# Five dense units moved from the kept steps into the list steps of a graph layer; tail roots and normalising one slot later

## The chip, the cores and the metric

The kernel runs on one core of one Trainium2 chip. The metric is the device time of one execution in microseconds (us); a lower time is better. Each time given as "median of the runs" is over unprofiled runs; the trace comes from one more execution, taken by the hardware profiler.

## What is computed

```python
x = setup()                         # (100000, 256) f32; 25000 edges, sorted by dst
def _spmm(edge_src, edge_dst, edge_weight, feats, n_nodes):
    msgs = edge_weight[:, None] * feats[edge_src]
    return jax.ops.segment_sum(msgs, edge_dst, num_segments=n_nodes)
feats = [x]; cur = x
for _ in range(3):
    cur = _spmm(src, dst, edge_weight, cur, n_nodes)
    feats.append(cur)
y = jnp.concatenate(feats, axis=1) @ shared_weight + output_bias   # weight (1024, 256)
out = layernorm(x + y)              # over the 256 columns, no gain or bias
```

Every node needs x times the first 256 rows of the weight, plus x, plus bias, and a layernorm: that is the **dense** part. Only nodes with edges need more, and only some edges reach a second and third hop: that is the **sparse** part, which ends in a gather and a scatter of single rows of the output.

## The kernel before

**Dense units.** The 100000 rows are cut into 195 units of 512 rows (128 partitions x 4 rows) and a tail. A unit is loaded by SP's queue (512 KB), turned on TensorE (`turn_pair`, L1472), copied to SBUF by ScalarE (`copy_xT`, L1185), multiplied on TensorE (`multiply_part`, L1483), copied out with the bias by VectorE (`copy_y`, L1840), measured there (`unit_stats`, L1846; `unit_end` with the lines 1855, 1851 and 1861), rooted and normalised by ScalarE (L1189, L1198) and stored by SP's queue (512 KB). A unit is two pairs, and each pair passes each of these engines once. VectorE's share of a unit is two `copy_y`, four `bn_stats` and three small instructions.

**Steps and slots.** The program is written out by hand, engine by engine, as steps of eight slots (q = 0 to 7). Each step carries a piece of the sparse part and a fixed number of dense units, which the tables of sizes set: one (ONE), two (PAIR), three (STEP) or four (FOUR). Within a step the tables `PAIR_AT`, `ROOTS_AT` and `ROWS_AT` say at which slot an engine does which pair. Every engine runs its own queue in that order and waits on semaphores; nothing is reordered at run time. The units go through the stages in one sequence:

- 25 `a` steps of two units (first hop, and the table of edges with a second hop);
- 10 **list steps** of one unit (`list_step`, L514). In the last six, five of which are called `LIST_STEPS`, the active edges are compacted into a list: VectorE makes indices for a group of 4 x 127 entries (`pass_tiles` L2213, `stage_list` L2223/L2224), POOL issues four indirect DMAs for it (`list_group` L973, the DMAs show as L917 with the tile `entries`), VectorE takes the landed entries (`take_entries` L2232 to L2240). Between these VectorE computes pointers in 40 small pieces (`find_pointers`, L2250 to L2301), each of which waits for the one before it;
- `bridge_b` (three units), five `b` steps of four units (second hop), `bridge_c`;
- ten `c` steps of one or two units (third hop; some early tail tiles), `bridge_d`;
- the **D steps** d = 3 to 23, four units each. A tile is 128 tails (last edge of a node). In the **kept steps**, d = 3 to 19, POOL gathers the eight tiles' rows from the stored output (`gather_d`, L917 tile `rows_in`), VectorE undoes their normalising and adds the sparse result (`c_restore` L2702), measures it (`c_stats` L2707, `group_squares` L2601, `group_variance` L2607), ScalarE takes the root for a group of four tiles (`c_roots` L1401), VectorE the inverse (`c_inverse` L2712), ScalarE normalises a tile (`c_normalise` L1408, output tile `u_out`), and POOL scatters it into the output (`scatter_d` L1110, shown as L921). From step 20 on the rows come from x and are turned and multiplied again on TensorE (L1751, L1757).

**Distances.** At slot n of the D steps (n = 8d + q) POOL issues the gather of tile n + 4 (which waits until tile n - 4 is restored) and the scatter of tile n - 12, which begins at n = 36, the middle of step 4; VectorE restores tile n - 2, which waits until ScalarE has normalised tile n - 10; ScalarE normalises tile n - 8, which waits for the scatters of the pair of tiles eight before it, since `u_out` holds eight tiles.

Of the kernel before, what the change touches and what calls it, by code (L numbers as in the profile page):

```python
def gnn_program(nc, x, src, dst, edge_weight, weight, bias, out):
# [23 lines left out]
    STEP = 3  # L25
    RING = 2 * STEP
    PAIR, FOUR = 2, 4
# [4 lines left out]
    G = 4  # L32
    Q = 2 * G
    FULL = E // EPT
    REST = E - FULL * EPT
    REAL = FULL + 1
# [16 lines left out]
    LIST_UNIT = A_UNIT + PAIR * A_STEPS  # L53
    LIST0 = 4
    LIST_STEPS = 5
    LIST_ALL = LIST0 + LIST_STEPS + 1
    ONE = 1
    B_UNIT = LIST_UNIT + ONE * LIST_ALL + STEP
    B_STEPS = LIST_STEPS
    BRIDGE_UNIT = B_UNIT + FOUR * B_STEPS  # L60
    FIRST_GROUPS = 2 * LIST_STEPS
# [4 lines left out]
    E_STEPS = E_QUADS * G // Q  # L66
    EARLY = Q * E_STEPS
# [4 lines left out]
    D_STEPS = REAL // Q  # L72
# [5 lines left out]
    GROUPS_MIN = FIRST_GROUPS + 1  # L78
    GROUPS_MAX = TILES // G
    LATE0 = Q * D_STEPS  # L80
    D_SIZES = (0,) * E_STEPS + (FOUR,) * (D_STEPS - E_STEPS)
    D_OFFS = tuple(D_UNIT + sum(D_SIZES[:d]) for d in range(D_STEPS))
    FRESH_UNIT = D_OFFS[KEPT_STEPS]
    assert D_UNIT + sum(D_SIZES) == UNITS

# [44 lines left out]
    with ctx:  # L130
# [202 lines left out]
        turns_at = {}  # L333
# [170 lines left out]
        def unit_at(off, turns=0):  # L504

            return off + RING * turns, off % RING, turns + off // RING, off % STEP
# [5 lines left out]
            return A_UNIT + PAIR * i, PAIR, turns, STEP if isinstance(turns, int) and i == 0 else PAIR  # L512

        def list_step(l):  # L514
            return LIST_UNIT + ONE * l, ONE, 0, PAIR

        def b_step(b):
            return B_UNIT + FOUR * b, FOUR, 0, FOUR if b > 0 else STEP


        bridge_b = (B_UNIT - STEP, STEP, 0, ONE)
        bridge_c = (BRIDGE_UNIT, STEP, 0, FOUR)
# [5 lines left out]
        def d_step(d):  # L528
            return D_OFFS[d], D_SIZES[d], 0, D_SIZES[d - 1] if d > E_STEPS else FOUR

# [639 lines left out]
        def _(act):  # L1170

            PAIR_AT = {FOUR: {q: q for q in range(Q)}, STEP: {0: 0, 1: 1, 2: 2, 4: 3, 5: 4, 6: 5},
                       PAIR: {0: 0, 2: 1, 4: 2, 6: 3}, 1: {0: 0, 4: 1}}

            ROOTS_AT = {FOUR: {1: -1, 3: 0, 5: 1, 7: 2}, STEP: {2: -1, 4: 0, 7: 1}, PAIR: {2: -1, 6: 0}, 1: {4: -1}}
            ROWS_AT = {FOUR: {0: (-3, 1), 1: (-2, 0), 2: (-2, 1), 3: (-1, 0), 4: (-1, 1), 5: (0, 0), 6: (0, 1), 7: (1, 0)},
                       STEP: {0: (-3, 1), 2: (-2, 0), 3: (-2, 1), 4: (-1, 0), 5: (-1, 1), 7: (0, 0)},
# [3 lines left out]
            def copy_xT(p, rows=P):  # L1181
                act.wait_ge(xT_psum, p + 1)
                until(act, y_psum, columns_before[p] + 1)
                view = [t[:, :].rearrange("p (q c) -> p q c", c=P)[:, :, 0:rows] for t in (columns_in[p], turned_in[p])]
                act.copy(view[0], view[1]).then_inc(xT_copied, 1)  # L1185

            def roots(u, k, rows=P, tiles=RPP):
                act.wait_ge(var_ready, u + 1)
                act.activation(std_all[0:rows, RPP * u:RPP * u + tiles], squares[k][0:rows, 0:tiles], ACT.Sqrt,  # L1189
                               scale=1.0 / D, bias=eps[0:rows, :]).then_inc(std_ready, 1)  # L1190

            def normalise(u, k, slot, turn, half, rows=P):

                if half == 0:
                    act.wait_ge(rstd_ready, u + 1)
                    until(act, stored[slot], 16 * turn)
                for r in (2 * half, 2 * half + 1):
                    last = act.activation(o_ring[slot][0:rows, r * D:(r + 1) * D], y_ring[k][0:rows, r * D:(r + 1) * D],  # L1198
                                          ACT.Copy, scale=rstd[k][0:rows, r:r + 1])
                if half == 1 or rows < P:  # L1200
                    last.then_inc(normed, 1)

            def dense_slot(dense, q):
                off, units, turns, before = dense

                def has_rows(i):

                    return i >= -off and (i > -3 or before >= STEP)

                if q in ROWS_AT[units] and ROWS_AT[units][q][0] == -3 and has_rows(-3):  # L1210
                    u, slot, turn, k = unit_at(off - 3, turns)
                    normalise(u, k, slot, turn, 1)
                if off >= D_UNIT:
                    if off == D_UNIT and q == 0:
                        copy_xT(LAST_PAIR)
                    for p in turns_at.get(2 * off + q, ()):
                        copy_xT(p)
                elif q in PAIR_AT[units]:
                    copy_xT(2 * off + PAIR_AT[units][q])
                if q in ROOTS_AT[units] and has_rows(ROOTS_AT[units][q]):  # L1220
                    u, slot, turn, k = unit_at(off + ROOTS_AT[units][q], turns)
                    roots(u, k)
                if q in ROWS_AT[units]:
                    i, half = ROWS_AT[units][q]
                    if i > -3 and has_rows(i):
                        u, slot, turn, k = unit_at(off + i, turns)
                        normalise(u, k, slot, turn, half)
# [134 lines left out]
            for n in range(G * FIRST_GROUPS):  # L1362
                g, k = n // G, n % G
# [39 lines left out]
            def c_normalise(n, q, group, turn):  # L1403
                act.wait_ge(crstd_ready, group + 1)
                if q % 2 == 0:
                    until(act, scattered[q // 2], 32 * turn)
                half, k = q // G, q % G
                act.activation(co[q], cy[q], ACT.Copy, scale=crstd[half][:, k:k + 1]).then_inc(cnormed, 1)  # L1408

            def step_d(d, slot=None):  # L1410

                for q in range(Q):
                    n, g = Q * d + q, 2 * d + q // G
                    if KEPT <= n < REAL:
                        copy_ta(n, q)
                    if slot is not None:
                        slot(q)
                    if q % G == 2 and 2 * E_STEPS < g <= -(-REAL // G):
                        c_roots(g - 1, (q // G + 1) % 2)
                    if Q + EARLY <= n < REAL + Q:  # L1420
                        c_normalise(n - Q, q, g - 2, d - 1)

            def last_units(q):
                u = UNITS
# [391 lines left out]
        def _(dve):  # L1816
# [545 lines left out]
            for b in range(LIST_STEPS):  # L2362
                dense = list_step(LIST0 + b)
                for q in range(Q):
                    g = 2 * b + 2 + q // G
# [9 lines left out]
            for q in range(G):  # L2375
                if q % 2 == 0:
                    g = FIRST_GROUPS - 2 + q // 2
# [247 lines left out]
            for n in range(G * FIRST_GROUPS):  # L2625
                g, k = n // G, n % G
# [32 lines left out]
            LAST_GROUP = (REAL - 1) // G  # L2659
# [49 lines left out]
            def c_inverse(g, half):  # L2709
                dve.wait_ge(cstd_ready, g + 1)  # L2710
                until(dve, cnormed, G * (g - 1))
                dve.reciprocal(crstd[half][:, :], cstd[half][:, :]).then_inc(crstd_ready, 1)  # L2712

            def step_d(d, par, turn, copies=None, measures=None):
                for q in range(Q):
                    n, g, half = Q * d + q, 2 * d + q // G, q // G
                    real = 2 + EARLY <= n < REAL + 2
                    measured = 3 + EARLY <= n < REAL + 3
                    if measured and (q % G == 2 or n == REAL + 2):
                        dve.wait_ge(cstats_ready, n - 2)  # L2720
                        group_squares((n - 3) // G, (n - 3) % G + 1)
                    if real:
                        before = q < 2
                        part = 2 * ((par + before) % 2) + (q - 2) % Q // G
                        if n - 2 < KEPT:
                            c_restore(n - 2, (q - 2) % Q, d - before, part, turn - 1 if before and par == 0 else turn)
                        else:
                            c_copy(n - 2, (q - 2) % Q, part, turn - 1 if before and par == 0 else turn)
                    if copies is not None:
                        copies(q)  # L2730
                    if n < KEPT and q < 2:
                        (pick_std, sum_picked)[q](d)
                    if real:
                        c_stats(n - 2, (q - 2) % Q)
                    for s in range(1, len(SPLITS)):
                        if SPLITS[s][0] == d and q < 4:
                            split_std(s, q)
                    if d + 1 < KEPT_STEPS and q in (2, 3):
                        mark_parts(d + 1, q - 2)
                    if d + 1 < KEPT_STEPS and q == 5:  # L2740
                        mark_cols(d + 1)
                    if measures is not None:
                        measures(q)
                    if measured and (q % G == 2 or n == REAL + 2):
                        group_variance((n - 3) // G, (n - 3) % G + 1)
                    if q % G == 3 and 2 * E_STEPS + 1 <= g <= LAST_GROUP + 1:
                        c_inverse(g - 1, 1 - half)

            last_step = (UNITS, STEP, 0, STEP)

# [72 lines left out]
```

## Time and profile before

| | us |
|---|---|
| median of 3 runs | 1538.12 (1538.0 to 1543.98) |
| the profiled execution | 1543.04, of which the span is 1541.0 |

| engine | busy us | share of the span |
|---|---|---|
| TensorE (PE) | 1417.6 | 92% |
| VectorE (DVE) | 1177.7 | 76% |
| POOL (GpSimd) | 1072.4 | 70% |
| ScalarE (ACT) | 998.6 | 65% |

The span is the time from the first to the last instruction, 2.0 us less than the execution's own time. The shares are averages over stages with very different limits. A DMA that POOL issues shows as an instruction of about 1 us on POOL, which is the issuing alone; what it moves shows in the DMA columns. In the views of time, an instruction's start is followed by how long it took; two instructions of one engine can overlap by some tens of ns, so the cost of one in a row of them is the distance from start to start.

### The profile page before, as it was taken

Reading aid. Unit: us, or ns where it says so; the run is one execution under the profiler, and the core shown is the slowest. Engines: PE = TensorE matmul, PEld = TensorE weight load, DVE = VectorE, ACT = ScalarE, POOL = GpSimd, SP = SyncE. Lnnn points to the kernel's source line nnn. Section 1 sums busy time; section 2 is a strip of 40 time slices with the busy share of each in tenths; the row PEclk is TensorE's granted clock in tenths of the full one; section 3 lists DMA queues with packets and bytes.
Section 4 is the critical chain, followed back from the end, with each engine's and each line's share of the span. In section 5 each row is a group of like instructions: output and inputs, shape, how many; then the busy total and the mean of one; then the engine's idle time right before and its main releaser. Section 6 shows DMA issues by size and latency. Waiting matters only on the chain. (4 is left out here: it accounts for less than half of the span.)

```text
span 1541.0 us, 29919 instructions
## 1 busy us (share of the span) xinstructions
PE 1417.6 (92%) x7990; PEld 1209.9 (79%) x7990; DVE 1177.7 (76%) x4195; ACT 998.6 (65%) x2674; POOL 1072.4 (70%) x1046
## 2 busy tenths in 40 slices
PE   6999999999999986689989999989998998888995
PEld 5888888888888875578878878878777777767884
DVE  8777777777777777978763766549999999997664
ACT  4677777777777753257764555646777776666665
POOL 4577777777777754747755877873777777777744
PEclk9999999999999999799999999999999999999997
DMA  7788988888888875378976877769999999998863
GB/s 260 248 259 275 281 280 281 266 272 282 281 279 265 274 239 182 99 237 311 334 271 166 239 231 199 205 175 326 341 349 344 342 338 337 332 338 295 301 204 124
DMA packets 214319, 410.69 MB, mean 267 GB/s; under 512 B 30996, under 2 KB 137485, under 8 KB 214154
## 3 DMA queue, kind: packets, MB, share of 16 engines
q1 hardware_dynamic: 164582, 311.03, 59.0%
q0 software_dynamic: 48576, 97.04, 22.2%
q8 instruction: 67, 1.10, 0.3%
q10 hardware_dynamic: 996, 0.72, 0.2%
q14 instruction: 98, 0.80, 0.2%
HBM read 227.02 MB, written 193.96 MB: 273 GB/s over the span
## 5 line engine op out<-in xcount | busy, mean ns | idle before, releaser
L1483 PE MATMUL ps_y<-w_sb,xT 128*128 128x256 f32 (+1 forms) x1928 | 501.3, 389 | 14.7 <-DVE y_ring L1840 12.5
L1483 PEld LDWEIGHTS ps_y<-w_sb,xT 128*128 128x128 f32 (+1 forms) x1928 | 353.3, 195 | 55.7 <-issue 9.1
L1198 ACT ACTIVATE o_ring<-y_ring,rstd 128x256 f32<-128x256 f32 (+1 forms) x782 | 350.3, 498 | 0.0
L1840 DVE TENSOR_TENSOR y_ring<-ps_y,bias 128x512 f32<-128x512 f32 (+1 forms) x325 | 224.0, 689 | 150.1 <-PE ps_y L1483 136.8
L1846 DVE BATCH_NORM_STATS2 stats<-y_ring 128x6 f32<-128x256 f32 (+1 forms) x782 | 291.2, 414 | 4.2
L917 POOL DMA_INDIRECT rows_in<-in_x,gather_idx x200 | 202.5, 1013 | 87.6 <-issue 66.5
L917 POOL DMA_INDIRECT tails_found<-tail_keys,table_idx x200 | 201.2, 1006 | 79.5 <-issue 58.2
L921 POOL DMA_INDIRECT out_rows<-u_out,early_node x173 | 178.4, 1031 | 80.6 <-issue 39.8
L917 POOL DMA_INDIRECT rows_in<-out_rows,early_node x160 | 166.9, 1043 | 73.2 <-issue 39.3
L1568 PE MATMUL ps_u<-w_sb,cT 128*128 128x256 f32 x788 | 206.2, 384 | 0.3 <-DVE u_out L2084 0.3
L1472 PE MATMUL ps_xT<-ident,x_ring 128*128 128x128 f32 x1140 | 177.8, 280 | 13.1 <-ACT xT L1185 8.0
L1247 ACT COPY rows_in<-ps_sum 1x256 f32<-1x256 f32 x282 | 101.1, 358 | 128.3 <-PE ps_sum L1546 73.3
L1185 ACT COPY xT<-ps_xT 128x512 f32<-128x512 f32 x254 | 145.3, 572 | 58.3 <-PE ps_xT L1472 58.2
L1472 PEld LDWEIGHTS ps_xT<-ident,x_ring 128*128 128x128 f32 x1140 | 140.2, 144 | 37.3 <-ACT xT L1185 10.7
L1483 PE MATMUL ps_sum<-w_sb,xT 128*128 128x256 f32 x528 | 138.6, 388 | 19.9 <-ACT xT L1185 19.9
L1568 PEld LDWEIGHTS ps_u<-w_sb,cT 128*128 128x128 f32 x788 | 141.8, 190 | 16.3 <-issue 1.0
L2084 DVE COPY u_out<-ps_u 128x512 f32<-128x512 f32 x80 | 55.3, 691 | 96.8 <-PE ps_u L1568 56.6
L1483 PEld LDWEIGHTS ps_sum<-w_sb,xT 128*128 128x128 f32 x528 | 93.8, 192 | 39.7 <-ACT xT L1185 30.6
L1546 PE MATMUL ps_sum<-rows_in,sels 128*128 128x256 f32 x394 | 119.9, 386 | 5.2 <-ACT rows_in L1247 4.3
L1189 ACT ACTIVATE std_all<-squares,eps 128x4 f32<-128x4 f32 x196 | 58.4, 298 | 90.1 <-DVE squares L1861 88.0
L1408 ACT ACTIVATE u_out<-sums,crstd 128x256 f32<-128x256 f32 x173 | 86.0, 500 | 44.5 <-DMA out_rows<-u_out,early_node 42.7
L1483 PE MATMUL ps_y<-w_sb,xT_more 128*128 128x256 f32 x336 | 89.5, 390 | 7.1 <-ACT xT_more L1185 7.0
(365 smaller groups left out, 2595.2 us busy)
## 6 DMA issues: line engine op xcount, KB each, us to landing
x_ring<-in_x SPq DMA_DIRECT2D x195, 512.0 KB, 5.9
out_rows<-o_ring SPq DMA_DIRECT2D x195, 512.0 KB, 4.4
c_rows<-sums SPq DMA_DIRECT2D x49, 512.0 KB
u_rows<-u_out SPq DMA_DIRECT2D x49, 512.0 KB, 5.1
keys_bc<-u_rows SPq DMA_DIRECT2D x21, 512.0 KB, 7.3
listed<-u_rows SPq DMA_DIRECT2D x14, 512.0 KB, 5.6
c_list_rows<-sums SPq DMA_DIRECT2D x11, 512.0 KB
u_out<-c_list_rows SPq DMA_DIRECT2D x44, 128.0 KB, 4.7
```

The lines of the kernel that those rows point to most:

```text
L917: pool.indirect_dma_start(dest, None, table, bass.IndirectOffsetOnAxis(ap=index, axis=0), bounds_check=bound, oob_is_err=False).then_inc(s ...
L921: pool.indirect_dma_start(table, bass.IndirectOffsetOnAxis(ap=index, axis=0), source, None, bounds_check=bound, oob_is_err=False).then_inc ...
L1185: act.copy(view[0], view[1]).then_inc(xT_copied, 1)
L1198: last = act.activation(o_ring[slot][0:rows, r * D:(r + 1) * D], y_ring[k][0:rows, r * D:(r + 1) * D], ACT.Copy, scale=rstd[k][0:rows, r:r ...
L1247: act.copy(rows_in[row][0:1, :], last_row).then_inc(carry_ready, tiles)
L1408: act.activation(co[q], cy[q], ACT.Copy, scale=crstd[half][:, k:k + 1]).then_inc(cnormed, 1)
L1472: last = pe.transpose(bank[:, q * P:q * P + rows], x_ring[slot][0:rows, at:at + P], ident[0:rows, 0:rows])
L1483: last = pe.matmul(y_bank[p][0:rows, r * D:(r + 1) * D], columns_in[p][:, q * P:q * P + rows], w_sb[:, c, :], start=c == 0, stop=c == KC - 1)
L1546: pe.matmul(ps_sum[e // 2 % 2][:, e % 2 * D:(e % 2 + 1) * D], sel[q % G][:, :], rows_in[q][:, :], start=True, stop=True).then_inc(summed, ...
L1568: last = pe.matmul(ps_u[1][:, r * D:(r + 1) * D], cT[j % 2][:, at:at + P], w_sb[:, KC + c, :], start=c == 0, stop=c == KC - 1)
L1840: dve.tensor_tensor(y_ring[k][0:rows, half * 2 * D:(half + 1) * 2 * D], y_bank[p][0:rows, :], bias2[0:rows, :], ALU.add).then_inc(y_copied, 1)
L1846: last = dve.bn_stats(stats[k][0:rows, r, :], y_ring[k][0:rows, r * D:(r + 1) * D])
```

## The change

Three edits go together.

1. The five `LIST_STEPS` carry two units instead of one (`L_SIZES`). All later stages up to the kept steps therefore work on units whose number is five higher; their sizes stay.
2. The kept steps 4, 8, 12, 16 and 19 carry three units instead of four (`LIGHT_STEPS`). For those ScalarE gets a table, `TURNED_AT`, of the slots at which TensorE has turned a pair. From step 20 on every unit stands where it stood.
3. On ScalarE the root of a group of tails moves from slot 2 (or 6) to slot 3 (or 7), and at slot n tile n - 9 is normalised instead of n - 8. On VectorE `c_inverse` is written at the start of a slot instead of at the end of the one before it, which is the same place in its queue.

```diff
+    L_SIZES = (ONE,) * LIST0 + (PAIR,) * LIST_STEPS + (ONE,)
-    B_UNIT = LIST_UNIT + ONE * LIST_ALL + STEP
+    B_UNIT = LIST_UNIT + sum(L_SIZES) + STEP
...
-    D_SIZES = (0,) * E_STEPS + (FOUR,) * (D_STEPS - E_STEPS)
+    LIGHT_STEPS = (4, 8, 12, 16, 19)
+    D_SIZES = (0,) * E_STEPS + tuple(STEP if d in LIGHT_STEPS else FOUR for d in range(E_STEPS, D_STEPS))
...
         def list_step(l):
-            return LIST_UNIT + ONE * l, ONE, 0, PAIR
+            return LIST_UNIT + sum(L_SIZES[:l]), L_SIZES[l], 0, PAIR
...
+            TURNED_AT = {FOUR: {q: q for q in range(Q)}, STEP: {1: 0, 2: 1, 3: 2, 5: 3, 6: 4, 7: 5}}
...
-                    for p in turns_at.get(2 * off + q, ()):
+                    done = TURNED_AT[units].get(q)
+                    for p in turns_at.get(2 * off + done, ()) if done is not None else ():
                         copy_xT(p)
...
-                    if q % G == 2 and 2 * E_STEPS < g <= -(-REAL // G):
+                    if q % G == G - 1 and 2 * E_STEPS < g <= -(-REAL // G):
                         c_roots(g - 1, (q // G + 1) % 2)
-                    if Q + EARLY <= n < REAL + Q:
-                        c_normalise(n - Q, q, g - 2, d - 1)
+                    m = n - Q - 1
+                    if EARLY <= m < REAL:
+                        c_normalise(m, m % Q, m // G, m // Q)
...
+                    if q % G == 0 and 2 * E_STEPS + 2 <= g <= LAST_GROUP + 2:
+                        c_inverse(g - 2, half)
...
-                    if q % G == 3 and 2 * E_STEPS + 1 <= g <= LAST_GROUP + 1:
-                        c_inverse(g - 1, 1 - half)
```

How VectorE's queue reads in the second half of a list step, first before (here `sums` and `own` are pieces of the pointers, `passes_out`, `entries` and `list_idx` the making of the indices, `y_ring`, `stats`, `rstd` and `squares` a dense unit):

```order
L2213 SCALAR_TENSOR_TENSOR passes_out,passed<-ends,position,skips 128x201 x4
L2273 TENSOR_TENSOR sums<-sums 128x256
L2223 COPY entries<-blank_entries 128x36
L2224 TENSOR_TENSOR list_idx<-list_row,passed 128x4
L2273 TENSOR_TENSOR sums<-sums 128x256 x2
L2276 SCALAR_TENSOR_TENSOR own,begun_before<-ident,sums 128x128
L1840 TENSOR_TENSOR y_ring<-ps_y,bias 128x512
L1846 BN_STATS stats<-y_ring 128x6 x2
L1855 SCALAR_TENSOR_TENSOR stats<-stats 128x8
```

and the same stretch of VectorE's queue after (line numbers are five higher):

```order
L2218 SCALAR_TENSOR_TENSOR passes_out,passed<-ends,position,skips 128x201 x4
L2278 TENSOR_TENSOR sums<-sums 128x256
L2228 COPY entries<-blank_entries 128x36
L2229 TENSOR_TENSOR list_idx<-list_row,passed 128x4
L2278 TENSOR_TENSOR sums<-sums 128x256
L1845 TENSOR_TENSOR y_ring<-ps_y,bias 128x512
L1851 BN_STATS stats<-y_ring 128x6 x2
L1860 SCALAR_TENSOR_TENSOR stats<-stats 128x8
L1856 RECIPROCAL rstd<-std_all 128x4
L1866 TENSOR_REDUCE squares<-stats 128x4
L2278 TENSOR_TENSOR sums<-sums 128x256
```

Every half step now holds two pairs of a dense unit where it held one; nothing else of VectorE's list work has gone.

ScalarE's queue in a kept step of four units, slots 2 to 4, before (`xT1` and the like are turned pairs, `o_ring` a dense unit's output, `cstd` the tails' root, `u_out` a normalised tail tile):

```order
L1198 ACTIVATE o_ring5<-y_ring2,rstd2 128x256 x2
L1401 ACTIVATE cstd1<-csquares1,eps 128x4
L1408 ACTIVATE u_out<-sums,crstd0 128x256
L1185 COPY xT1<-ps_list 128x512
L1189 ACTIVATE std_all<-squares1,eps 128x4
L1198 ACTIVATE o_ring0<-y_ring0,rstd0 128x256 x2
L1408 ACTIVATE u_out<-sums,crstd0 128x256
```

and after:

```order
L1201 ACTIVATE o_ring5<-y_ring2,rstd2 128x256 x2
L1412 ACTIVATE u_out<-sums,crstd0 128x256
L1188 COPY xT_more<-ps_list 128x512
L1192 ACTIVATE std_all<-squares1,eps 128x4
L1201 ACTIVATE o_ring0<-y_ring0,rstd0 128x256 x2
L1405 ACTIVATE cstd1<-csquares1,eps 128x4
L1412 ACTIVATE u_out<-sums,crstd0 128x256
```

The tails' root stands behind the next turned pair and the next dense root, and so does what follows it.

## Rows read from the trace of the kernel before

**Rows 1.** Busy time by stretch: list steps, kept steps, last steps (x instructions).
```profile
core 0: us, PE busy (x) PEld busy (x) DVE busy (x) ACT busy (x) POOL busy (x), PEclk, DMA share, GB/s
601.00:659.00 58.00, 36.65 (x144) 27.88 (x144) 54.99 (x244) 17.68 (x42) 44.46 (x44) 0.85 0.37 106
1077.00:1398.00 321.00, 287.93 (x1799) 236.95 (x1798) 309.98 (x968) 226.68 (x575) 248.26 (x239) 0.99 0.97 339
1404.00:1515.00 111.00, 110.26 (x601) 95.94 (x602) 75.68 (x244) 75.04 (x197) 66.16 (x67) 0.98 0.73 247
```

**Rows 2.** Waits in the list steps, 601 to 659: total us, times, longest.
```profile
DVE sums L2255 <- DVE next_f L2253: 0.5, 1, 0.5
...
POOL entries L917 <- DVE list_idx L2224: 13.5, 1, 13.5
POOL entries L917 <- issue: 13.1, 43, 0.3
```

**Rows 3.** VectorE in a list step, a unit's first pair, and another unit's second.
```profile
635.13 0.69 DVE L1840 TENSOR_TENSOR y_ring<-ps_y,bias 128x512 f32<-128x512 f32 x1
...
636.52 0.15 DVE L2232 SCALAR_TENSOR_TENSOR key_in<-entries 128x4 f32<-128x4 f32 x1
...
640.32 0.69 DVE L1840 TENSOR_TENSOR y_ring<-ps_y,bias 128x512 f32<-128x512 f32 x1
...
642.12 0.15 DVE L2232 SCALAR_TENSOR_TENSOR key_in<-entries 128x4 f32<-128x4 f32 x1
```

**Rows 4.** Waits of POOL and of VectorE in the kept steps, 1077 to 1398.
```profile
POOL rows_in L917 <- issue: 27.9, 91, 0.3
POOL out_rows L921 <- issue: 27.7, 91, 0.3
...
POOL rows_in L917 <- ACT u_out L1408: 3.3, 10, 0.6
...
DVE sums L2702 <- ACT u_out L1408: 6.4, 7, 2.5
```

**Rows 5.** POOL in step 4, where the scatters begin, in order of time.
```profile
1073.26 1.00 POOL L917 DMA_INDIRECT rows_in<-out_rows,early_node  x1 [1.58 <-DVE sums L2702]
1074.56 1.02 POOL L921 DMA_INDIRECT out_rows<-u_out,early_node  x1 [0.30 <-issue]
1076.13 1.03 POOL L917 DMA_INDIRECT rows_in<-out_rows,early_node  x1 [0.55 <-ACT u_out L1408]
```

**Rows 6.** VectorE in a kept step, a unit's second pair and what follows it.
```profile
1185.04 0.74 DVE L1846 BATCH_NORM_STATS2 stats<-y_ring 128x6 f32<-128x256 f32 x2
1185.71 0.15 DVE L2601 SCALAR_TENSOR_TENSOR cstats<-cstats 128x8 f32<-128x8 f32 x1
...
1186.17 0.68 DVE L1840 TENSOR_TENSOR y_ring<-ps_sum,bias 128x512 f32<-128x512 f32 x1
1186.77 0.41 DVE L2707 BATCH_NORM_STATS2 cstats<-sums 128x6 f32<-128x256 f32 x1
1187.11 0.73 DVE L1846 BATCH_NORM_STATS2 stats<-y_ring 128x6 f32<-128x256 f32 x2
1187.87 0.17 DVE L1855 SCALAR_TENSOR_TENSOR stats<-stats 128x8 f32<-128x8 f32 x1
...
1188.16 0.16 DVE L2607 TENSOR_REDUCE csquares<-cstats 128x4 f32<-128x16 f32 x1
```

**Rows 7.** The first VectorE instruction of kept steps 4, 7 and 19.
```profile
1067.46 0.61 DVE L2669 TENSOR_TENSOR sels<-ps_u,matches 128x448 f32<-128x448 f32 x1
...
1128.49 0.61 DVE L2669 TENSOR_TENSOR sels<-ps_u,matches 128x448 f32<-128x448 f32 x1
...
1383.49 0.62 DVE L2669 TENSOR_TENSOR sels<-ps_u,matches 128x448 f32<-128x448 f32 x1
```

**Rows 8.** The chain that ended last, where the kept steps end: start, us, what.
```profile
1397.67 7.03 DMA rows_in<-in_x,tail_node
...
1404.74 0.69 PE ps_u L1751 x2
```

## The prediction

> **What bounds the kernel now.** I read the busy time of the stretches that the change touches first, then who waited for whom in each, then the order of time at the places where one engine hands over to another.
>
> *The list steps* [rows 1] take 58 us. VectorE is busy for 54.99 us of them, so it is full. POOL is nearly full too, in another way: it issues 44 gathers of list entries, busy 44.46 us, plus a fixed 0.3 us between two of them, 13.1 us in all [rows 2], together 57.6 us. After the first gather it never waits for VectorE (the 13.5 us stand before that gather), and VectorE's one wait of note is 0.5 us [rows 2]; its whole idle time is 58 - 54.99 = 3.0 us. So two engines run through this stage side by side at the same pace, and neither has room. TensorE has: 36.65 us of 58. ScalarE has: 17.68.
>
> *The kept steps* [rows 1] look full everywhere: VectorE 309.98 of 321 us, TensorE 287.93, DMA share 0.97 at 339 GB/s. What orders them is the waits. POOL issues 239 DMAs in 321 us, one each 1.343 us; 248.26 us are busy, and its waits are the same 0.3 us before every instruction, whatever released it [rows 4]. The longest is 0.6 us. It is the 0.3 us that also stands between list gathers that wait for nothing, so it is the price of an issue and no wait. POOL has therefore no idle moment from 1077 to 1398 us. A kept step has 16 of its instructions (8 gathers, 8 scatters), which makes 16 x 1.343 = 21.5 us. VectorE alone would be faster: from step 4 to step 7 a step took (1128.49 - 1067.46) / 3 = 20.34 us, and from step 7 to step 19 (1383.49 - 1128.49) / 12 = 21.25 us [rows 7]. In the first part POOL fell behind by using up its lead; in the second VectorE was held to POOL's pace, through ScalarE, which waits for scatters to land before it overwrites a tile (VectorE's 6.4 us in 7 waits for `u_out` [rows 4]).
>
> *The last steps* begin when POOL's gather of tile 160, the first row of step 20, has landed: issued at 1397.67, 7.03 us under way, and TensorE starts at 1404.74 [rows 8]. From there TensorE is full, 110.26 of 111 us [rows 1]. So the chain to the end is: list steps, a TensorE-full stage, the third hop, POOL from 1077 to 1398, TensorE from 1405.
>
> **The list steps after.** Each of five steps gets one unit more. VectorE pays for a unit's first pair 636.52 - 635.13 = 1.39 us and for its second, with the three small instructions, 642.12 - 640.32 = 1.80 us, start to start [rows 3], so 3.19 us for a unit and 5 x 3.19 = **15.95 us** in all. I place all of it on the path, because VectorE's only real gap is that 0.5 us. Its bounds: if all 3.0 us of idle time were filled, 13.0; if it cost what it costs in a kept step (below), 14.6; if it met a new wait of up to the 0.5 us above in each step, 18.5. Of the other engines none is late: POOL's 57.6 us become less than VectorE's 58 + 16 = 74; TensorE's 36.65 us grow with its instructions, 5/10 more dense work even if all of it were dense and at half clock twice that, to at most 36.65 x 2 = 73, and the granted clock was 0.85 here, so it is more likely near 55; ScalarE doubles to 35 at most. The 10 added transfers of 512 KB make 5.2 MB beside the 106 GB/s x 58 us = 6.1 MB of now, in 74 us, 154 GB/s, less than half of the 339 of the kept steps. The gathers of entries and the indices that VectorE makes two groups ahead of POOL now wait for VectorE instead of the other way about; that is where the queue behind the added work shows. The pointers, the entries and everything behind them start some 16 us later. If POOL set this stage alone, the added work would be hidden; the busy time of VectorE speaks against it.
>
> **The kept steps after.** A unit costs VectorE there 0.60 + 0.67 us for the first pair (a copy start to start, 1186.77 - 1186.17, and the measuring, 1185.71 - 1185.04) and 0.60 + 0.76 + 0.29 for the second (1187.87 - 1187.11, 1188.16 - 1187.87) [rows 6], 2.92 us. Five units are 14.6 us of VectorE's time, and about as much of TensorE's. Only what VectorE was late with counts. Before the first scatter POOL waited for VectorE at every gather: 1.58 us at 1073.26, and 0.55 us still at 1076.13 [rows 5]. Those gathers wait for tiles 32 and 33, restored in slots 2 and 3 of step 4. In a light step slot 0 has no pair, so one pair less stands ahead of them: 1.27 us for the first, 1.65 for the second. POOL's own spacing then allows 1073.26 - 1.27 + 2 x 1.30 = 1074.6 instead of 1076.13, which is **1.5 us** gained. From there POOL issues without a wait, as now; the rest of step 4's unit and the whole of the units of steps 8, 12, 16 and 19, 13.1 us of VectorE's time, turn into waiting of VectorE and TensorE for POOL. Bounds: nothing gained at all, 0; everything, 14.6. I take 1.5, since the saved pairs after 1077 have no reader that was late for them.
>
> **Roots and normalising one slot later.** This has one cover: POOL's pace. ScalarE normalises tile n - 9 at slot n, still before POOL scatters n - 12, so POOL does not wait. VectorE restores n - 2 one slot after ScalarE has finished n - 10, where it had two slots. A slot is 21.25 / 8 = 2.66 us, and ScalarE's work in it, 226.68 us in some 121 slots, is 1.9 us, so it is just in time. For the other sign: ScalarE no longer stands at slot 2 for a root that VectorE finishes at the end of slot 2, and has one slot more for a scatter to land. I count 0; if each of the 34 groups of four tiles met one wait like the mean of the seven of now (6.4 / 7 = 0.9 us), 31 us would be added to VectorE, of which POOL's lead hides 15 x 0.9 us and the light steps 11.7, leaving up to 6. In the last steps the tail tiles are normalised by the same queue in the same order; between 0 and one slot of TensorE's, 3.25 us, I take 0, since VectorE is busy there 75.68 of 111 us.
>
> **Sum**, against the profiled execution: 1543.04 + 15.95 - 1.5 + 0 = 1557.5 us, so +14.4. The median of the runs is 4.9 us below that execution; 1538.1 + 14.4 gives **1552.5 us**, +0.94%.
>
> **A rule that speaks for the change.** The kept steps move 339 GB/s with a DMA share of 0.97 [rows 1]. If the bytes set their pace, each unit taken out (512 KB in, 512 KB out, 1.049 MB) gives 1.049 / 0.339 = 3.1 us, five of them 15.5. The Trainium skill, "DMA: Bandwidth & Descriptors", Specifications, puts the limit of the memory per core at about 358 GB/s, of which the measured 339 is 95%; by that rule the kept steps are bound by bandwidth. It is rival A below, under its own price. What speaks against it is POOL's row: an engine that issues each DMA 0.3 us after the last has not been held by transfers, and it has the larger sum.
>
> **The rivals.**
> A. *The kept steps give it back.* VectorE, TensorE or the bytes set the pace there, and POOL only follows. Then 14.6 to 15.5 us return: 1538.1 + 15.95 - 14.6 = 1539.5 (1538.6 by the bytes), no change. For it: VectorE's 97% and the DMA share. Against it: steps 7 to 19 ran 0.9 us slower than VectorE can. It decides from the point where POOL's 21.5 us a step fall below VectorE's 20.3.
> B. *The list steps hide it*, VectorE's pieces of pointers being in truth paced by the landing of entries: then the stage stays at 58 us and the time is 1536.6, or 1523.5 with A. Against it: no wait on `entries` is listed for VectorE.
> C. *The later normalising stalls the restores*, up to 6 us more: 1558.5.
> D. *Half of A*, POOL slack in part: about 1545.5.
>
> **Chances.** The forecast 0.70 (1547 to 1557), A 0.09 (1536 to 1543), D 0.07 (1543 to 1547), B 0.06 (1522 to 1538), C 0.08 (1556 to 1562). The range 1540 to 1557 leaves out B, most of C and part of A, about 0.17. About 0.5% (7.7 us, 1530.4 to 1545.8) is what a measurement of this kernel can tell from no change. Slower by more: the forecast, C and half of D, 0.80. Within it: A, the rest of D and a part of B, 0.15. Faster by more: B with A, 0.05.
>
> **What would show it.** In the changed kernel's profile the list steps should take about 74 us instead of 58, with VectorE full and POOL waiting for `list_idx` in most groups. In the kept steps POOL should again show only 0.3 us before each instruction, 16 instructions a step at 21.3 to 21.6 us, with VectorE's and TensorE's idle time up by some 13 us together with waits for `u_out` or for landed rows; the distance from the first scatter to the gather of tile 160 should be what it was, 1397.67 - 1074.56 = 323 us. The wait of TensorE for tile 160 should be longer. Wrong would be the forecast if that distance fell by more than 5 us (A), if the list steps grew by less than 10 us (B), or if POOL showed waits for `u_out` of over 0.3 us in the kept steps (C).

## The result, and the profile after

| | before | after |
|---|---|---|
| median of the runs, us | 1539.18 (1534.91 to 1544.06, 6 runs) | 1555.54 (1553.32 to 1558.34, 6 runs) |
| the profiled execution, us (its span) | 1543.04 (1541.0) | 1556.87 (1554.8) |

The changed kernel is slower: the ratio is 1.0098, with a 95% interval from 1.0081 to 1.0115, some 15 us (the two medians lie 16.4 us apart). The forecast was +14.4 us and 1552.5 us.

I cut both traces at the same five events and compare the pieces. (`sels` is the instruction of [rows 7]; in a step whose slot 0 holds a dense pair, the copy of that pair stands 0.6 us ahead of it.) The pieces add up to the difference of the two spans, 13.8 us.

| piece, from and to | before | after | difference | forecast |
|---|---|---|---|---|
| start to the first `list_idx` of the list | 599.65 | 601.36 | +1.7 | 0 |
| list: to the last `take_entries` | 62.10 | 77.77 | **+15.67** | +15.95 |
| second and third hop: to the `sels` instruction of step 3 on VectorE | 386.63 | 385.49 | -1.1 | 0 |
| to the first scatter (step 4) | 26.18 | 24.93 | **-1.25** | -1.5 |
| kept steps: first scatter to the gather of tile 160 | 323.11 | 322.32 | **-0.8** | 0 |
| gather of tile 160 to the end | 143.33 | 142.93 | -0.4 | 0 |

*The list steps.* Busy time by stretch after, which answers to [rows 1]: list steps, kept steps, last steps.

```profile
core 0: us, PE busy (x) PEld busy (x) DVE busy (x) ACT busy (x) POOL busy (x), PEclk, DMA share, GB/s
603.00:676.00 73.00, 53.17 (x263) 42.40 (x264) 69.55 (x285) 32.42 (x77) 43.84 (x44) 0.98 0.50 155
1092.00:1412.00 320.00, 275.76 (x1698) 228.79 (x1696) 299.04 (x931) 217.47 (x548) 247.27 (x239) 0.96 0.95 330
1419.00:1530.00 111.00, 111.00 (x611) 96.46 (x609) 78.30 (x250) 74.72 (x196) 65.09 (x65) 0.99 0.71 237
```

And the waits from 603 to 677 us after, which answer to [rows 2] (total us, times, longest):

```profile
POOL entries L919 <- DVE list_idx L2229: 25.3, 7, 14.2
...
POOL entries L919 <- issue: 11.5, 37, 0.5
...
DVE sums L2260 <- DVE next_f L2258: 0.5, 1, 0.5
```

VectorE is busy for 69.55 of 73 us and still has one wait, of 0.5 us. Its idle time is 3.45 us, where it was 3.0 of 58: the added work filled no gap and met no new wait. POOL changed sides. Before, one wait of 13.5 us stood ahead of its first gather and nothing but 0.3 us behind it; now it waits seven times for the indices, and 25.3 - 14.2 = 11.1 us of that lie behind the first gather. TensorE (36.65 to 53.17) and ScalarE (17.68 to 32.42) took their share in idle time that they had. VectorE after, a whole unit and then a unit's second pair (start, us), as in [rows 3]:

```profile
631.08 0.68 DVE L1845 TENSOR_TENSOR y_ring<-ps_y,bias 128x512 f32<-128x512 f32 x1
...
634.27 0.15 DVE L2237 SCALAR_TENSOR_TENSOR key_in<-entries 128x4 f32<-128x4 f32 x1
...
636.52 0.69 DVE L1845 TENSOR_TENSOR y_ring<-ps_y,bias 128x512 f32<-128x512 f32 x1
...
638.32 0.41 DVE L2275 COPY sums<-ps_sum 128x255 f32<-128x255 f32 x1
```

A unit, 634.27 - 631.08 = 3.19 us, costs here what [rows 3] gave; its second pair, 638.32 - 636.52 = 1.80 us, too.

*The kept steps.* Waits from 1092 to 1412 us after, which answer to [rows 4]:

```profile
ACT std_all L1192 <- DVE squares L1866: 71.9, 51, 2.3
...
POOL rows_in L919 <- issue: 27.9, 91, 0.3
POOL out_rows L923 <- issue: 27.1, 89, 0.3
...
DVE sums L2707 <- ACT u_out L1412: 16.0, 17, 2.3
...
POOL rows_in L919 <- ACT u_out L1412: 4.0, 13, 0.3
```

POOL issues the same 239 DMAs and never waits longer than the 0.3 us that stand before every one of them. Its own pace stayed: from its gather of tile 60 to that of tile 156, twelve steps, a step took 21.58 us before (1127.82 to 1386.81) and 21.57 after (1142.28 to 1401.06). VectorE has 320 - 299.04 = 21.0 us idle where it had 11.0, and its waits for `u_out` have grown from 6.4 to 16.0 us: the same 10 us. TensorE's idle time went from 33.1 to 44.2 us. So the work that left became waiting for POOL. The handovers, on POOL, VectorE and TensorE, which answer to [rows 5], [rows 7] and [rows 8]:

```profile
1083.09 0.62 DVE L2674 TENSOR_TENSOR sels<-ps_u,matches 128x448 f32<-128x448 f32 x1
1142.97 0.61 DVE L2674 TENSOR_TENSOR sels<-ps_u,matches 128x448 f32<-128x448 f32 x1
1397.07 0.62 DVE L2674 TENSOR_TENSOR sels<-ps_u,matches 128x448 f32<-128x448 f32 x1
```

```profile
1088.25 1.00 POOL L919 DMA_INDIRECT rows_in<-out_rows,early_node  x1 [1.99 <-DVE sums L2707]
1089.55 1.24 POOL L923 DMA_INDIRECT out_rows<-u_out,early_node  x1 [0.30 <-issue]
...
1411.87 1.02 POOL L919 DMA_INDIRECT rows_in<-in_x,tail_node  x1 [0.31 <-issue]
...
1417.48 0.69 PE L1756 MATMUL ps_u<-ident,rows_in 128*128 128x128 f32 x2 [6.71 <-DMA rows_in<-in_x,tail_node]
```

On VectorE the `sels` of steps 4, 7 and 19 begin at 1083.09, 1142.97 and 1397.07. From 7 to 19 a step took 21.18 us, with three light steps (8, 12 and 16) among the twelve, where it was 21.25 with none. Of these 0.9 us in all, 0.6 are the copy of a pair that light step 19 lacks ahead of its `sels`. From the first scatter to the gather of tile 160 are 322.32 us. That is 0.8 us less than before, and no gain can be read from it: the kernels below that keep four units in every kept step and POOL's queue as it is (the third edit alone, the fewer bytes, and the three of the last two experiments) took 320.5 to 322.5 us over the same piece. TensorE waits 6.71 us for the row of tile 160, where it waited 2.93.

### The profile page after: what moved, and what is told of

Its sections match the earlier page's. It is cut to its first block and busy times, and to the rows that moved or that the text cites. A ratio compares the mean times of both kernels' runs of the same rounds, so it can differ in the third digit from the quotient of the medians.

```text
span 1554.8 us, 29919 instructions
## 1 busy us (share of the span) xinstructions
PE 1416.8 (91%) x7990; PEld 1212.0 (78%) x7990; DVE 1179.5 (76%) x4195; ACT 1001.6 (64%) x2674; POOL 1068.7 (69%) x1046
## 5 line engine op out<-in xcount | busy, mean ns | idle before, releaser
L1488 PE MATMUL ps_y<-w_sb,xT 128*128 128x256 f32 x2496 | 645.7, 388 | 31.4 <-ACT xT L1188 24.4
L1488 PEld LDWEIGHTS ps_y<-w_sb,xT 128*128 128x128 f32 x2496 | 453.8, 194 | 87.5 <-ACT xT L1188 32.1
L1845 DVE TENSOR_TENSOR y_ring<-ps_y,bias 128x512 f32<-128x512 f32 (+1 forms) x331 | 228.0, 689 | 144.1 <-PE ps_y L1488 130.9
L1477 PE MATMUL ps_xT<-ident,x_ring 128*128 128x128 f32 x1164 | 180.8, 279 | 22.0 <-ACT xT L1188 16.4
L1188 ACT COPY xT<-ps_xT 128x512 f32<-128x512 f32 x261 | 149.5, 573 | 70.7 <-PE ps_xT L1477 70.6
L1477 PEld LDWEIGHTS ps_xT<-ident,x_ring 128*128 128x128 f32 x1164 | 141.8, 143 | 47.8 <-ACT xT L1188 21.5
L1239 ACT ACTIVATE sign_out<-first_keys,source_key 128x197 bf16<-128x197 f32 x200 | 90.6, 453 | 0.0
L1049 POOL DMA_INDIRECT u_rows<-u_out,scatter_idx x44 | 70.3, 1598 | 23.8 <-issue 14.7
L1551 PEld LDWEIGHTS ps_sum<-rows_in,sels 128*128 128x128 f32 x394 | 73.2, 192 | 16.0 <-issue 5.0
```

The costliest lines, as they stand in the source:

```text
L1477: last = pe.transpose(bank[:, q * P:q * P + rows], x_ring[slot][0:rows, at:at + P], ident[0:rows, 0:rows])
L1488: last = pe.matmul(y_bank[p][0:rows, r * D:(r + 1) * D], columns_in[p][:, q * P:q * P + rows], w_sb[:, c, :], start=c == 0, stop=c == KC - 1)
L1551: pe.matmul(ps_sum[e // 2 % 2][:, e % 2 * D:(e % 2 + 1) * D], sel[q % G][:, :], rows_in[q][:, :], start=True, stop=True).then_inc(summed, ...
L1845: dve.tensor_tensor(y_ring[k][0:rows, half * 2 * D:(half + 1) * 2 * D], y_bank[p][0:rows, :], bias2[0:rows, :], ALU.add).then_inc(y_copied, 1)
```

## The experiments

Ratios are to the kernel before on the same chip, with a 95% interval. Times of pieces are from one profiled execution each, cut as in the table above. Where nothing is said of the list, it took 62.0 to 62.1 us with one unit a step and 77.7 with two.

**The third edit alone.** The kernel before, with roots and normalising one slot later and no unit moved.

```diff
-                    if q % G == 2 and 2 * E_STEPS < g <= -(-REAL // G):
+                    if q % G == G - 1 and 2 * E_STEPS < g <= -(-REAL // G):
                         c_roots(g - 1, (q // G + 1) % 2)
-                    if Q + EARLY <= n < REAL + Q:
-                        c_normalise(n - Q, q, g - 2, d - 1)
+                    m = n - Q - 1
+                    if EARLY <= m < REAL:
+                        c_normalise(m, m % Q, m // G, m // Q)
...
```

> The kernel before with only the third edit: tail roots and normalising one slot later. My theory (POOL's issuing covers ScalarE's order): no change, within 2 us. Rival C (the restores stall on the later normalising): up to 6 us slower, with VectorE waiting for u_out at most groups. A gain of over 3 us would say that the roots' stalls on ScalarE had been on the path.

1541.69 us, ratio 1.000 (0.9986 to 1.0014). The edit costs nothing and gains nothing, within 2 us. Yet the trace shows that it moved waits about; from 1077 to 1398 us:

```profile
ACT std_all L1189 <- DVE squares L1862: 75.2, 60, 2.2
...
ACT u_out L1408 <- DMA out_rows<-u_out,early_node: 10.3, 13, 1.7
...
DVE sums L2703 <- ACT u_out L1408: 5.0, 8, 1.5
```

ScalarE's wait for landed scatters was 40.9 us in 26 before and is 10.3 now, and its 49.5 us of waiting for the tails' squares (25 waits of `cstd`) are gone from the list; it waits for dense squares instead, 75.2 us for 1.4. VectorE's wait for `u_out` is 5.0 us where it was 6.4. Rival C, a stall of the restores by this edit, is out for the kernel before.

**The moved units alone.** The changed kernel with the third edit taken back.

```diff
-                    if q % G == G - 1 and 2 * E_STEPS < g <= -(-REAL // G):
+                    if q % G == 2 and 2 * E_STEPS < g <= -(-REAL // G):
                         c_roots(g - 1, (q // G + 1) % 2)
-                    m = n - Q - 1
-                    if EARLY <= m < REAL:
-                        c_normalise(m, m % Q, m // G, m // Q)
+                    if Q + EARLY <= n < REAL + Q:
+                        c_normalise(n - Q, q, g - 2, d - 1)
...
```

> The changed kernel without the third edit: only the five units move. My theory: all of the loss is here, +14 to +16 us against the kernel before, list steps some 16 us longer, kept steps at most 1.5 us shorter. If the later normalising had been part of the loss (or of a hidden gain), this run is faster (or slower) than the changed kernel by that.

1555.07 us, ratio 1.0081 (1.006 to 1.0102). The list took 77.74 us, the piece to the first scatter 24.94 (26.18 before) and the kept steps 321.43. The whole loss is in the moved units; what the third edit adds to them is 0.0017 in the ratio (1.0098 - 1.0081), inside either interval.

**One small DMA more on POOL in each kept step.** If POOL has no idle moment, a DMA that nobody needs must lengthen the stage by its issue.

```diff
                         scatter_d(n - LAG, (q + G) % Q, d - back, (par + back) % 2)
+                    if q == Q - 1 and 5 <= d < KEPT_STEPS:
+                        pool.wait_ge(list_in[0], 16 * G * 3 + 16 * (d - 5))
+                        limit(P * TILES)
+                        gather(entries[0][:, 0:FIELDS], list_dram, list_idx[0][:, 0:1], list_in[0])
```

> The kernel before with one more indirect DMA on POOL in each of the 15 kept steps from 5 to 19, which gathers 128 rows of 36 bytes (4.6 KB, nobody reads them). POOL theory: each costs its full issue, 15 x 1.34 = +20 us. If VectorE or the bytes set the pace (rival A), next to nothing, under +3 us, until POOL's slack of theirs is used up.

1560.03 us, ratio 1.0123 (1.0098 to 1.0147). The kept steps took 341.64 us for 323.11, with 14 DMAs more up to the gather of tile 160: 18.5 / 14 = 1.32 us each. The whole execution took 17 to 19 us more, for the 20 expected. POOL around one of them:

```profile
1217.69 1.01 POOL L921 DMA_INDIRECT out_rows<-u_out,early_node  x1 [0.30 <-issue]
1219.01 1.29 POOL L917 DMA_INDIRECT entries<-listed_edges,list_idx  x1 [0.31 <-issue]
1220.60 1.00 POOL L917 DMA_INDIRECT rows_in<-out_rows,early_node  x1 [0.30 <-issue]
```

The added DMA moves little, but it costs a full issue, 1220.60 - 1219.01 = 1.59 us at this place and 1.32 in the mean, and none of it is hidden. This alone doesn't tell whether less work on POOL would help; the next but one does.

**Fewer bytes.** The 56 units from step 6 to step 19 load only one of each partition's four rows, 128 KB for 512, 22 MB less in all. The rest of these units is computed from what the buffer held, so that part of the output is not the layer's.

```diff
-                sp.dma_start(x_ring[slot][:, :], unit_rows(x, u)).then_inc(x_loaded[slot], 16)
+                if D_OFFS[6] <= u < D_OFFS[KEPT_STEPS]:
+                    rows = x[bass.ds(u * UROWS, UROWS), :].rearrange("(p r) d -> p r d", r=RPP)
+                    sp.dma_start(x_ring[slot][:, 0:D].rearrange("p (r d) -> p r d", r=1), rows[:, 0:1, :]).then_inc(x_loaded[slot], 16)
+                else:
+                    sp.dma_start(x_ring[slot][:, :], unit_rows(x, u)).then_inc(x_loaded[slot], 16)
```

> The kernel before, with 56 units of the kept steps loading a quarter of their rows (128 KB instead of 512 KB; the other rows are what the buffer held, so part of the output is computed from old rows). 22 MB less are moved, every engine's instructions stay. POOL theory and VectorE theory: no change, within 3 us. If the bytes set the pace of the kept steps: 22 MB at 339 GB/s would be 65 us, of which VectorE's 20.34 us a step lets 11 to 12 us through: -11 us or more.

1540.7 us, ratio 0.9989 (0.9973 to 1.0004), and the kept steps took 322.02 us. The same stretch, 1095 to 1375 us, of the kernel before and then of this one:

```profile
1095.00:1375.00 280.00, 252.04 (x1590) 207.65 (x1590) 270.93 (x847) 198.81 (x504) 216.43 (x209) 0.99 0.97 340
```

```profile
1095.00:1375.00 280.00, 256.28 (x1622) 212.99 (x1622) 273.87 (x857) 202.18 (x513) 216.43 (x209) 0.99 0.82 269
```

The DMA share fell from 0.97 to 0.82 and the rate from 340 to 269 GB/s, and POOL issued the same 209 DMAs in the same 280 us. The bytes don't set the pace.

**Half of the scatters left out, in the kernel before.** From tile 41 to tile 151 every other scatter isn't issued, 56 of them, so that POOL has room; the rows of those tiles keep what the dense part wrote.

```diff
-                scatter(out[:, :], co[q], early_node[:, n:n + 1], scattered[q // 2])
+                if q % 2 == 1 and Q * 5 <= n < KEPT - Q:
+                    pool.reg_add(bound, nought, N - 1)
+                elif q % 2 == 0 and Q * 5 <= n < KEPT - Q:
+                    pool.indirect_dma_start(out[:, :], bass.IndirectOffsetOnAxis(ap=early_node[:, n:n + 1], axis=0), co[q], None,
+                                            bounds_check=bound, oob_is_err=False).then_inc(scattered[q // 2], 32)
+                else:
+                    scatter(out[:, :], co[q], early_node[:, n:n + 1], scattered[q // 2])
```

> The kernel before without the scatters of every second tail tile from tile 41 to 151 (56 indirect DMAs left out; those rows keep their dense value). POOL then has 12 instructions a step, 16.1 us. POOL theory: the pace falls to VectorE's 20.34 us a step, 0.9 us less in each of steps 7 to 19, -11 us, and no further, since VectorE is next. If VectorE set the pace already: 0 to -2 us.

1530.26 us, ratio 0.9921 (0.9895 to 0.9947), 11 to 12 us less, as expected. Its kept steps took 306.14 us with 187 DMAs for 239. Busy time and POOL's first wait from 1095 to 1375 us, and two step starts of VectorE:

```profile
1095.00:1375.00 280.00, 257.70 (x1641) 213.25 (x1641) 278.10 (x875) 203.77 (x519) 178.21 (x171) 1.00 0.96 332
```

```profile
POOL rows_in L917 <- DVE sums L2708: 48.8, 40, 1.9
```

```profile
1212.24 0.62 DVE L2675 TENSOR_TENSOR sels<-ps_u,matches 128x448 f32<-128x448 f32 x1
...
1252.96 0.61 DVE L2675 TENSOR_TENSOR sels<-ps_u,matches 128x448 f32<-128x448 f32 x1
```

Now POOL waits for VectorE, in 40 places, and VectorE is busy for 278.10 of 280 us. Two steps took 40.72 us, 20.36 each, which is the 20.34 of [rows 7] that the prediction took for VectorE's own pace. 52 DMAs less are 70 us of POOL's time, of which the stage got 17: VectorE stands right behind POOL. ScalarE's waits for landed scatters and VectorE's for `u_out` are both gone from the list of waits of this window. The 17 us have two parts. VectorE's twelve steps from 7 to 19 took 8.7 us less (20.53 a step in the mean, for 21.25). And POOL, which in the kernel before issued its gather of tile 156 3.3 us after VectorE's `sels` of step 19, issued it here 4.2 us ahead of it, 7.5 us more. The piece behind the gather of tile 160 grew by 3.2 us (143.33 to 146.50), which is why the whole execution gained 12 us and not 17.

**The same scatters left out of the changed kernel.** If POOL's pace was what held the light steps' gain back, this kernel must come close to the one before it.

```diff
+                if q % 2 == 1 and Q * 5 <= n < KEPT - Q:
+                    pool.reg_add(bound, nought, N - 1)
...
```

> The changed kernel with the same 56 scatters left out. With POOL out of the way its light steps should now give back their units: against e5 +16 us for the list steps and -14.6 us for the kept steps, so e6 and e5 within 3 us of each other, where the changed kernel and the kernel before are 15 us apart. If the light steps are worth little whatever POOL does, e6 stays 12 to 16 us above e5.

1535.81 us, ratio 0.9962 (0.9945 to 0.998): 5.5 us above the last experiment, where the same change cost 15 to 16 us with all scatters. The kept steps took 298.55 us for 306.14, the piece to the first scatter 24.94 for 26.18: 8.8 us came back. From 1095 to 1375 us:

```profile
1095.00:1375.00 280.00, 250.00 (x1596) 208.71 (x1594) 276.04 (x864) 198.83 (x507) 183.63 (x176) 0.99 0.96 329
```

```profile
POOL rows_in L919 <- ACT u_out L1418: 39.4, 33, 1.8
...
DVE sums L2713 <- ACT u_out L1418: 2.0, 3, 0.7
```

```profile
1171.32 0.48 DVE L2713 SCALAR_TENSOR_TENSOR sums<-rows_in,row_std,keys_bc 128x256 f32<-128x256 f32 x1 [0.68 <-ACT u_out L1418]
```

So with room on POOL more than half of the light steps' 14.6 us comes back, and with POOL full hardly any does. The size was missed: I expected this kernel within 3 us of the other, so 13 us or more back. A light step gave back about 2 us where the sum had 2.92. VectorE is no longer quite full (4.0 us idle in 280, for 1.9), and the list names where: it now waits three times for ScalarE's `u_out`, 0.7 us each, once in each of the light steps 8, 12 and 16 (the row above is step 8), where the last experiment lists no such wait. From the `sels` of step 7 to that of step 18, with these three light steps between them, VectorE took 219.66 us for 225.49, 5.8 less where 3 x 2.92 = 8.8 were to come; the waits make up 2.0 of the 2.9 us that are missing. POOL stands for `u_out` in 33 places, where it stood for VectorE; the left-out scatters still wait for their tile, so part of these waits belongs to them. That the later normalising is behind both is likely, since it sets when `u_out` is ready, but it isn't shown: no kernel had light steps, half of the scatters and the old order.

**Units taken from where TensorE is full.** The kernel before, with two units moved from steps 22 and 23 into the first two steps of the third hop, where TensorE has idle time. As in the change, ScalarE gets the table `TURNED_AT` for the lighter steps.

```diff
-    C_SIZES = (ONE,) * E_GROUP + (PAIR,) * (FIRST_GROUPS - E_GROUP)
+    C_SIZES = (PAIR,) * FIRST_GROUPS
...
-    D_SIZES = (0,) * E_STEPS + (FOUR,) * (D_STEPS - E_STEPS)
+    LIGHT_STEPS = (22, 23)
+    D_SIZES = (0,) * E_STEPS + tuple(STEP if d in LIGHT_STEPS else FOUR for d in range(E_STEPS, D_STEPS))
...
```

> A placing that the readings favour: from the kernel before, two units leave the last steps 22 and 23, where TensorE is full (110.26 of 111 us), for the first two c steps, which hold one unit each; VectorE is busy 58% of that stage. A unit costs TensorE 12 x 0.217 = 2.6 us in the last steps, so -5.2 us there. Cost in the c steps between 0 (their VectorE and POOL have room) and 5 us (TensorE is busy 92% of that stage): -5 to 0 us in all; if the c steps' chain of gather, sum and scatter pays for every instruction put into it, +1 to +3 us.

1538.94 us, ratio 0.9984 (0.9964 to 1.0003), which leaves open whether there is a gain, so I ran it once more.

> The kernel before with two dense units moved out of steps 22 and 23 into the first two steps of the third hop, once more, since the first comparison (ratio 0.9984, 0.9964 to 1.0003) could not tell a small gain from none. The trace of the first had the stage ahead of the kept steps 5.1 us longer and the last steps 11.7 us shorter. If that difference is real: 1533 to 1537 us where the kernel before has 1541, a ratio of 0.995 to 0.9975. If it was the spread of one profiled execution: 1539 to 1541, a ratio of 0.999 to 1.0.

1538.31 us (11 runs), ratio 0.9982 (0.9972 to 0.9993): a gain, but of 3 us, less than that expectation's 4 to 8. The last piece of the second trace, from the gather of tile 160, before and in this kernel:

```profile
1398.00:1541.00 143.00, 122.38 (x650) 104.09 (x648) 89.86 (x295) 90.32 (x238) 84.85 (x84) 0.92 0.66 225
```

```profile
1401.00:1535.00 134.00, 111.70 (x592) 95.24 (x592) 83.87 (x273) 85.36 (x224) 84.58 (x84) 0.92 0.66 223
```

TensorE's busy time fell by 10.7 us and the piece by 9.5 (143.33 to 133.82), so nearly all of it was on the path. A unit was thus worth 5 us there, twice the 2.6 us of the first of these two expectations: the trace has 58 matmul records less for two units, 29 each, where I had counted 12. The stage of the second and third hop grew by 3.7 us (5.1 in the first trace). By these two the gain should be 6 us. The runs give 3, and one trace can't tell more, as the next experiment shows.

**The lighter steps elsewhere.** As the last, with the two lighter steps 20 and 21.

```diff
-    LIGHT_STEPS = (22, 23)
+    LIGHT_STEPS = (20, 21)
```

> As the one before, but the two lighter steps are 20 and 21, right behind the gather of tile 160, instead of 22 and 23. If the last steps are a stretch in which TensorE is full from its first instruction, the place of the lighter steps does not matter and the time is that of the other within 1.5 us. If TensorE waits in steps 20 and 21 for rows that POOL gathers (one tile each 2.7 us), a lighter step there buys nothing but that wait: 3 to 6 us slower than the other, about 1540 to 1542.

1541.32 us (12 runs), ratio 0.9993 (0.9981 to 1.0005). The piece behind the gather of tile 160 took 133.74 us, against 133.82 with steps 22 and 23, so for this piece the place of the lighter steps doesn't matter and TensorE is full from the first of them on. The medians differ by 3.0 us all the same, more than the 1.5 I allowed, though the intervals overlap. By the time alone, 1541.32 us would be what I had expected if TensorE waited in steps 20 and 21; the trace is what speaks against that reading. In this trace the stage of the second and third hop took 397.48 us, 7.1 more than in the trace of the last kernel, over code that is the same in both.

## Why the prediction was right

**List steps, +15.95: measured +15.67.** The step from "VectorE has one gap of 0.5 us" to "all of it is on the path" held, with the price per unit, and so did what would show it: 77.74 us again with the units alone, POOL waiting for `list_idx`, TensorE near 55 us (53.17), 154 GB/s (155). One working there was off: TensorE's instructions didn't grow by 5/10 but nearly doubled (x144 to x263 between the marks), and one took 0.20 us for 0.25, with a granted clock of 0.98 in this stage where it was 0.85. I had named the stage 58 us between round marks; by its own events it went from 62.10 to 77.77. Rival B is out: nothing was hidden.

**Kept steps, -1.5 and no more: measured -1.25, and -0.8 that is within the spread.** The 1.25 us came where it was said, in step 4 ahead of the first scatter; the kernels with and without the third edit show 24.93 and 24.94 us there. From there on the argument was that a row of 0.3 us waits with mixed releasers is an engine without an idle moment. The extra gather and the halved scatters show that from both sides: one DMA more costs 1.32 us, and fewer speed the stage up until VectorE holds it at 20.36 us a step. VectorE's share of 97% in [rows 1] was no sign of a bound; it was 1 us a step from being one. That nearness is why halving POOL's scatters gave 17 us and not 70. The 21.25 us a step that the prediction took for VectorE held to POOL's pace are a mixture: POOL took 21.58 a step, and VectorE came close to that only from step 13 on, (1383.49 - 1253.51) / 6 = 21.66 us, when POOL was 2 to 4 us behind it. The idle time of VectorE and of TensorE grew by 10.0 and 11.1 us, less than the some 13 that it was said to.

**The rule that spoke for the change.** A DMA share of 0.97 at 339 GB/s was the best argument for rival A. With 22 MB less the stage kept its length, so the share was that of engines kept busy, and no limit that was reached. The Trainium skill, "DMA: Bandwidth & Descriptors", Specifications, gives 358 GB/s; the same page, under Measured, calls that the share when both cores of a pair stream, and has 425 GB/s for one core alone. That figure is for one large load. By it the kept steps were at 80%, and that the bytes set no pace there agrees with it; no run here shows where the limit is.

**Rivals A and D** fell with the 0.8 us of the kept steps. With half of the scatters left out, the light steps bring 8.8 us back: A, in its form with VectorE, was the right mechanism for a kernel in which POOL has room.

**Later roots and normalising, 0: measured 0** (0.9986 to 1.0014), so nothing of it came through. The measured median, 1555.54 us, lies just below rival C's 1556 to 1562, so the time alone hardly tells the two apart; the traces do, with the whole loss in the list steps and no wait of POOL over 0.3 us. That POOL's pace was the cover fits the changed kernel with half of the scatters, where POOL and VectorE do wait for `u_out`, the prediction's sign of C; no run shows it with the third edit alone.

**The sum.** By the traces +13.8 against +14.4; the parts that the change touches make 15.67 - 1.25 - 0.8 = +13.6. The rest is spread: the start of the list, +1.7, and the stage of the hops, -1.1, lie over code whose length the change leaves alone, and the kernel of the last experiment has +1.6 at the start of the list with nothing changed ahead of it. The 1552.5 us were 3.0 below the measured median, 1.1 of it because the kernel before had a median of 1539.18 in the comparison and not 1538.12, the rest within the interval of the ratio. Of the chances, the forecast, C and half of D add up to 0.815, not to the 0.80 that was written.

## What to carry to other kernels

Ask of a stage which engine's sum of issue and busy time has no idle moment, and take work out of that one. Here the change took work from two engines that waited for POOL and put it on VectorE in a stage where VectorE was full, so it paid the full price, some 16 us, and got between 1 and 2 us back. A DMA on POOL's queue counts with its start-to-start distance: 16 in a step of 21.5 us set a pace that neither 97% on VectorE nor 97% on the DMA engines set. And the units that were worth moving were those of the last steps, where TensorE was full: 5 us or so each there, against a price in the third hop that the traces put between 2 and 5 us each. The whole came to 3 us in one of the two placings, and to no gain clear of the noise in the other.

## What I had not expected

- A DMA share of 0.97 that was no bound: 22 MB less took it to 0.82, the rate from 340 to 269 GB/s, and the time moved by less than the interval (0.9973 to 1.0004).
- The same code took 390.34 us in one profiled execution and 397.48 in another, in the stages of the second and third hop. The list steps in the same traces took 62.06 and 62.03, and the piece to the first scatter 26.18 and 26.17. The kept steps, which POOL's queue filled, took 320.5 to 323.1 us in the six traces in which their work is the same. So a piece of these traces is good to 0.1 us where one engine is full of fixed work, to 2 or 3 us in the kept steps, and to some 7 us where hops wait for each other. The cause is open.
- ScalarE's wait for landed scatters fell by 30 us (40.9 to 10.3) with the third edit and the time stayed. Its wait for the tails' squares (49.5 us) went too, and 75.2 us of waiting for dense squares took the place of both. It was idle time of an engine that was not the bottleneck.
